# A transformer block on one core: attention outputs turned in 32x32 squares on VectorE instead of on TensorE, and the cross output projection moved into the next period

## What is computed

```python
def _attn(x, ctx, wq, wk, wv, wo, bo, heads):
    q = (x @ wq).reshape(b, n, heads, dh).transpose(0, 2, 1, 3)
    k = (ctx @ wk)...; v = (ctx @ wv)...
    a = jax.nn.softmax(jnp.einsum('bhid,bhjd->bhij', q, k) * scale, axis=-1)
    out = jnp.einsum('bhij,bhjd->bhid', a, v).transpose(0, 2, 1, 3).reshape(b, n, heads * dh)
    return out @ wo + bo
h1 = _ln(x, n1_g, n1_b); x = _attn(h1, h1, q1, k1, v1, o1_w, o1_b, heads) + x
h2 = _ln(x, n2_g, n2_b); x = _attn(h2, context, q2, k2, v2, o2_w, o2_b, heads) + x
h3 = _ln(x, n3_g, n3_b); a, g = split(h3 @ ff_w1 + ff_b1, 2)
return a * gelu(g) @ ff_w2 + ff_b2 + x
```

## Time and profile before

| what | value |
|---|---|
| median of three runs | 1340.88 us |
| the profiled execution: its span | 1337.6 us |
| TensorE busy / weight loads | 1292.3 us (97%) / 1203.1 us (90%) |
| VectorE busy | 814.5 us (61%) |
| ScalarE busy | 673.2 us (50%) |
| GpSimd busy | 612.5 us (46%) |
| a period of the attention part | 24.89 us, 29 of them |

### The profile page before, as it was taken

The page is one execution under the profiler, slowest core; times in us unless marked ns, Lnnn a source line. Parts: engine busy times, 40 slices in busy tenths (PEclk is TensorE's granted clock), DMA queues, the critical chain, the costliest instruction groups (busy, mean ns, idle before and its releaser), DMA issues. The chain is left out here.

```text
span 1337.6 us, 35594 instructions
## 1 busy us (share of the span) xinstructions
PE 1292.3 (97%) x13364; PEld 1203.1 (90%) x13364; DVE 814.5 (61%) x1729; ACT 673.2 (50%) x1558; POOL 612.5 (46%) x723
## 2 busy tenths in 40 slices
PE   5999789999999999999999999999889999999999
PEld 3999769999999999999999999998689999999999
DVE  5645367777777777777777777776665334242421
ACT  4665236566566566566566565565553232313131
POOL 5521324564564564654654654644356242333331
PEclk8999889999999999999999999999899999999999
DMA  4676644345345455455444354352111101010000
GB/s 125 223 253 215 206 130 145 116 147 153 120 142 155 141 158 162 142 162 166 134 148 149 121 162 132 122 157 95 42 56 48 45 1 50 0 49 0 25 1 25
DMA packets 118995, 154.59 MB, mean 116 GB/s; under 512 B 22336, under 2 KB 112696, under 8 KB 118840
## 3 DMA queue, kind: packets, MB, share of 16 engines
q1 hardware_dynamic: 118840, 152.49, 36.9%
HBM read 62.98 MB, written 28.93 MB: 69 GB/s over the span
## 5 line engine op out<-in xcount | busy, mean ns | idle before, releaser
L1398 ACT ACTIVATE probs<-expin 120x400 f32<-120x400 f32 (+2 forms) x635 | 297.8, 505 | 119.1 <-PE expin L753 106.4
L1075 DVE TENSOR_REDUCE neg_max<-score 100x2 f32<-100x722 f32 x320 | 289.6, 905 | 61.6 <-PE score L727 59.7
L1584 POOL MEMSET qs<- 1x2400 f32 (+1 forms) x116 | 224.2, 1933 | 17.2 <-PE attn L776 9.4
L753 PE MATMUL expin<-qs,ks 128*120 128x200 f32 (+2 forms) x1270 | 216.0, 276 | 2.6 <-ACT probs L1398 1.7
L753 PEld LDWEIGHTS expin<-qs,ks 128*120 128x120 f32 (+2 forms) x1270 | 178.0, 180 | 14.2 <-issue 4.4
L727 PE MATMUL score<-ks,qs 128*100 128x362 f32 x640 | 167.5, 343 | 6.0 <-DVE neg_max L1075 4.7
L1612 POOL TENSOR_TENSOR ctx_hi<-ctx_raw,one 128x480 fp32r<-128x480 f32 (+1 forms) x62 | 49.0, 790 | 260.2 <-PE work L693 239.8
L2594 DVE SCALAR_TENSOR_TENSOR hidden<-ps_a,b_cols,gelu 128x320 f32<-128x320 f32 x100 | 55.1, 551 | 163.5 <-PE ps_a L2518 159.1
L2756 POOL TENSOR_TENSOR hid_lo<-hidden,hid_hi 128x320 fp32r<-128x320 f32 x100 | 89.1, 892 | 120.6 <-ACT hid_hi L2664 120.4
L2676 ACT ACTIVATE gelu<-ps_g,b_cols 128x320 f32<-128x320 f32 x100 | 52.7, 527 | 134.3 <-PE ps_g L2518 134.3
L727 PEld LDWEIGHTS score<-ks,qs 128*100 128x100 f32 x640 | 84.8, 166 | 23.3 <-issue 8.7
(11 more groups left out here) (220 smaller groups left out, 2965.3 us busy)
## 6 DMA issues: line engine op xcount, KB each, us to landing
ks<-kc_parts SPq DMA_DIRECT2D x192, 181.0 KB, 2.8
qk_dram<-qk_parts SPq DMA_DIRECT2D x32, 500.0 KB, 5.3
qs<-q_parts SPq DMA_DIRECT2D x192, 75.0 KB
ks<-qk_dram SPq DMA_DIRECT2D x96, 125.0 KB
ctx_raw<-in_ctxT SPq DMA_DIRECT2D x64, 180.5 KB
ks<-kc_parts SPq DMA_DIRECT2D x96, 90.5 KB, 2.3
qs<-qk_dram SPq DMA_DIRECT2D x64, 125.0 KB
v_dram<-v_rows SPq DMA_DIRECT2D x32, 132.8 KB
```

What stands on the lines that cost most here:

```text
L753: mm = pe.matmul(dst, ks[a][u][:, c, j0:j0 + n], qs[a][u][:, :, q_slot(c) if a == 2 else c, :], start=True, stop=True)
L1075: ins = nc.vector.tensor_reduce(dst, src, AX_X, ALU.max, negate=True)
L1398: nc.scalar.activation(probs[e % NPT][0:n, :], expin[e % 2][0:n, 0:HG * N], ACT.Exp, scale=SCALE)\
L1584: link(nc.gpsimd.memset(row, 0.0))
```

## The change

The two turns on TensorE are gone. `copy_heads` on ScalarE copies `attn` in two instructions (400 and twice 100 columns) into a tile of 128 x 640, so that the columns fall into squares of 32. VectorE turns each 32x32 square of it (`turn_heads`, 640 columns) and takes 20 reciprocals; GpSimd multiplies (`scale_products`, 320 columns); VectorE turns the squares back (`turn_back`, 320 columns). The result has features in partitions, with the heads in another order, and ScalarE and GpSimd split it into high and low parts (`heads_high` from SBUF, `heads_low`). One set of these tiles serves both attentions in turn. The rows of the output weights are loaded in the new order of heads (`head_rows`, 24 DMAs of each of two matrices instead of 3), and the first stage turns the first item's heads the same way.

The cross output projection of x moves from the end of its period to the front of the next (`y = x - 1`), ahead of the second own score; `result` and `store_x2` move with it. The own output projection and keys part 1 change places, and so do the matching steps on VectorE. GpSimd clears a whole stack with one instruction instead of two rows with two, and SP's loads into the stack wait for that. In the drain the split of the feed-forward's weights stands behind the heads of the last items.

```diff
+def copy_heads(nc, pv, attn):
+    src = attn[:, 0:4 * N].rearrange("p (k s n) -> p k s n", k=2, s=2)
+    dst = pv[:, :, 0:4 * N - N].rearrange("p s (k n) -> p k s n", n=N)[:, 0:3:2]
+    nc.scalar.copy(dst, src)
+    last = attn[:, 4 * N:5 * N].unsqueeze(1).broadcast_to([P, 2, N])
+    return nc.scalar.copy(pv[:, :, N:2 * N], last)
+def scale_heads(engine, scaled, turned, rden):
+    src = turned[:].rearrange("p (s b r) -> p b s r", s=2, r=BLK)[:, :, :, 0:DH]
+    factor = rden[:].rearrange("p (s b) -> p b s", s=2).unsqueeze(3).broadcast_to([P, NB_HW, 2, DH])
+    return engine.tensor_tensor(scaled[:].rearrange("p (b s d) -> p b s d", s=2, d=DH), src, factor, ALU.mult)
...
 # TensorE, period
+                y = x - 1 if x else None
                 self_scores(f, 0)
...
                 scores_for_exp(1, c, 3, 0)
+                project_out(2, y)
                 self_scores(f, 1)
...
                 scores_for_exp(2, x, 0, 1)
-                turn_outputs(1, c, 0)
                 turn_max(1, f)
                 scores_for_exp(2, x, 0, 2)
-                turn_outputs(1, c, 1)
                 scores_for_exp(2, x, 1, 0)
...
                 times_v(2, x, 0)
-                turn_heads(1, c)
                 scores_for_exp(2, x, 1, 2)
                 scores_for_exp(2, x, 2, 0)
                 cross_scores(s, 2)
-                project_out(1, c)
+                project_kc(c, 1)
                 scores_for_exp(2, x, 2, 1)
                 scores_for_exp(2, x, 2, 2)
                 cross_scores(s, 3)
-                project_kc(c, 1)
+                project_out(1, c)
                 scores_for_exp(2, x, 3, 0)
                 scores_for_exp(2, x, 3, 1)
                 project_kc(c, 2)
                 cross_scores(s, 4)
...
                 project_q2(c)
-                turn_outputs(2, x, 0)
                 cross_scores(s, 7)
                 project_vc(c, 1)
-                turn_outputs(2, x, 1)
                 turn_q2(c)
                 cross_scores(s, 8)
-                turn_heads(2, x)
                 project_vc(c, 2)
                 cross_scores(s, 9)
-                project_out(2, x)
                 turn_max(2, s)
 # VectorE
-            def divide(a, b, i):
...
+            def turn_heads(a, b):
...
+                dve.wait_ge(pv_copied, n + 2)
+                dve.wait_ge(heads_lo_made, n + 1)
+                m = link(nc.vector.transpose(turned[:], pv[:].rearrange("p s c -> p (s c)")))
+                dve.wait_ge(dve_step, m)
+                invert_sums(nc, rden, turned).then_inc(heads_turned, 1)
+            def turn_back(a, b):
...
+                dve.wait_ge(heads_scaled, n + 1)
+                nc.vector.transpose(dense[:], scaled[:]).then_inc(heads_dense, 1)
 # VectorE, period
                 kc_low(c, 0)
+                result(y)
                 maximum(2, s, 0)
-                divide(1, c, 0)
-                divide(1, c, 1)
+                turn_heads(1, c)
                 maximum(2, s, 1)
                 max_low(1, f)
-                features_low("OT1", c)
+                turn_back(1, c)
                 maximum(2, s, 2)
+                kc_low(c, 1)
                 second_input(c)
                 maximum(2, s, 3)
                 normalise(c)
                 maximum(2, s, 4)
-                kc_low(c, 1)
                 maximum(2, s, 5)
...
                 maximum(2, s, 6)
-                divide(2, x, 0)
+                turn_heads(2, x)
                 maximum(2, s, 7)
-                divide(2, x, 1)
                 maximum(2, s, 8)
                 q2_low(c)
-                features_low("OT2", x)
+                turn_back(2, x)
                 maximum(2, s, 9)
                 max_low(2, s)
-                result(x)
 # ScalarE
             def heads_high(a, b):
...
+                act.wait_ge(heads_dense, n + 2)
+                before = OUT_BEFORE.get(n - 1, (1, 0))
+                act.wait_ge(*filled((f"O{before[0]}", before[1], 0)))
+                nc.scalar.copy(t_hi["OT"][:], thirds_of_heads(dense)).then_inc(heads_hi_made, 1)
 # GpSimd, run_out
+                scale_products(2, 31)
+                heads_low(2, 31)
                 for i in range(EARLY):
                     split_piece(i)
 # GpSimd, period
+                scale_products(1, c)
+                heads_low(1, c)
                 clear_own(p + 4 if p + 4 < B else None)
                 inverse_deviation(c)
-                split_context(f)
-                clear_cross(c)
                 second_residual(c)
                 first_residual(f)
+                clear_cross(c)
+                scale_products(2, x)
+                split_first(f)
+                heads_low(2, x)
+                split_last(f)
 # SP, first stage
+            def head_rows(dst, w, done):
+                for p0, k, src in rows_of_heads(w):
+                    sp.dma_start(dst[p0:p0 + DH, k, :], src).then_inc(done, 16)
```

More of the change, by code:

```diff
@@ L105 @@
 OWN_STEPS = [("scores", 0), ("scores", 1), ("max", 0)] + [("exponents", g) for g in range(G)]
-OWN_STEPS += [("values", g) for g in range(G)] + [("outputs", 0), ("outputs", 1), ("heads", 0)]
+OWN_STEPS += [("values", g) for g in range(G)]
 OWN_FULL = {step: n + 1 for n, step in enumerate(OWN_STEPS)}
 PROBS_AT, INPUT_AT = 27552, 43904
+LEAD_ROOM = 128
 @dataclass
@@ L209, with rows_of_heads @@
 PV_AT = {job: i for i, job in enumerate(PV)}
+CLEARED = [job for p in PERIODS for job in ((1, p + 4), (2, p + 2)) if job[1] < B] + [(2, B - 1)]
+CLEARED_AT = {job: i + 1 for i, job in enumerate(CLEARED)}
+HEADS_AT = {(a, b): i // G for (a, b, g), i in PV_AT.items() if g == 0}
+OUT_BEFORE = {n: (a, b) for (a, b), n in HEADS_AT.items()}
 def thirds_of(w):
     return [w[0:P], w[P:C].unsqueeze(0).broadcast_to([2, 64, w.shape[1]])] + ([w[C:D]] if w.shape[0] == D else [])
+def rows_of_heads(w):
+    pieces = []
+    for k, f0, step in ((0, 0, 4 * DH), (2, P, 4 * DH), (1, 2 * P, 0)):
+        for i in range(HG):
+            for half in range(2):
+                f = f0 + half * step + DH * i
+                pieces.append((BLK * i + DH * half, k, w[f:f + DH]))
+    return pieces
 def rows3(w):
@@ L652, in project_q2 @@
                     return
-                project(("Q2", b, 0), "T2", ("T2", b, 0), (hi_made["T2"], b + 1), [w_q2[:, i, :] for i in range(6)])
+                project(("Q2", b, 0), "T2", (hi_made["T2"], b + 1), emptied(("T2", b, 0)), [w_q2[:, i, :] for i in range(6)])
             def turn_q2(b):
@@ L1403, in copy_product @@
                     return
+                n = HEADS_AT[a, b]
                 act.wait_ge(pv_made, PV_AT[a, b, G - 1] + 1)
-                if b > (a == 1):
-                    act.wait_ge(*filled((f"OX{a}", b - 1, 1)))
-                nc.scalar.copy(pv[a][:], attn[:, 0:G * N]).then_inc(pv_copied, 1)
+                if n:
+                    act.wait_ge(heads_turned, n)
+                else:
+                    act.wait_ge(keys_set, 32)
+                copy_heads(nc, pv, attn).then_inc(pv_copied, 1)
             def heads_high(a, b):
@@ L1579, in inverse_deviation, with clear_stack @@
                 nc.gpsimd.tensor_tensor(rstd[:], var_eps[:], neg_half[0:N, :], ALU.pow).then_inc(rstd_made, 1)
-            def clear_rows(stack, landed):
-                for r in (0, 64):
-                    row = stack[r:r + 1].rearrange("p a c n -> p (a c n)").bitcast(F32)
-                    link(nc.gpsimd.memset(row, 0.0))
+            def clear_stack(stack, landed):
+                link(nc.gpsimd.memset(stack.rearrange("p a c n -> p (a c n)").bitcast(F32), 0.0))
+                pool.sem_inc(max_cleared, 1)
                 pool.sem_inc(landed, 16)
@@ L1929, in own_values @@
                 mm.then_inc(own_full, 1)
-            def turn_outputs(i):
-                pe.wait_ge(pv_copied, 1)
-                c0, c1 = XB[i]
-                for c in range(c0, c1):
-                    mm = pe.transpose(turn[i][0:N, (c - c0) * P:(c - c0 + 1) * P], ahead.pv[:, c * N:(c + 1) * N], identf[:])
-                mm.then_inc(own_full, 1)
-            def turn_heads():
-                pe.wait_ge(heads_made, 2)
-                pe.wait_ge(qk_lo_made, LAST + 1)
-                for k in range(3):
-                    mm = pe.transpose(qk_ps[2][:, k * N:(k + 1) * N], ahead.oh[:, k * P:(k + 1) * P], identf[0:N, 0:N])
-                mm.then_inc(own_full, 1)
             def turn_max():
@@ L1986, in _ @@
             values(NK - 1, 0)
-            for i in range(2):
-                turn_outputs(i)
-            values(NK - 1, 1)
-            values(NK - 1, 2)
-            turn_heads()
-            values(NK - 1, 3)
+            for i in range(1, NB):
+                values(NK - 1, i)
         @block.vector
@@ L2152, in _ @@
                 if k == NK - 1:
-                    for i in range(2):
-                        divide(i)
+                    normalise_heads()
                     heads_low()
@@ L2351, in _ @@
             pool.wait_ge(lo_made, B)
```

(1 more changed line is left out.)

259 lines of the change are left out of this document (133 added, 126 removed), and 8 rows, old and new, of tables (DRAIN_WORK, FILL_WORK).

## The result

The changed kernel took 1478.21 us in the median of four runs (1477.44 to 1483.67), the kernel before 1338.45 in the same series. The ratio is 1.107, with a 95% interval of 1.103 to 1.110. The profiled execution has a span of 1475.5 us against 1337.6, so 137.9 us more. They lie here, by the starts of the turn of the cross maxima that ends each period: 4.6 us more until the first of them (192.11 against 187.50), 114.1 more in the 29 periods (840.8 against 726.7), 17.8 more from there to the feed-forward (81.9 against 64.1), and 1.4 in the feed-forward.

A forecast was written before the change was run, and what follows sets the result against it. TensorE's list was taken to bound the 29 periods. Terms sum to +2.79 us a period, +81, plus 10.5 in the drain and 2 in the first stage: +94, giving 1434 us; range 1378 to 1485.

The forecast's parts named there:

- turns removed from TensorE: TensorE's list in each period: two turns to items by rows and one to features, per attention, go; -1.66 us.
- end of the period: Product 6 to next own scores: product and maximum rounds lack cover, 6.54 us against 4.95 of work; +1.76 us (1.59 to 2.1).
- maximum 3 behind the second input: Middle of the period: TensorE waits ahead of product 4, as VectorE's second input waits for the own output projection; +1.09 us.
- ScalarE's front: Front half of the period: split copy and wait at the heads' high parts make exponentials late; +0.9 us (0 to 1.4).
- normalisation beside GpSimd: VectorE's normalisation overlaps GpSimd's moved second residual sum, so maximum 4 is late; +0.30 us (0 to 0.47) a period.
- context's last piece: GpSimd's last context split stands behind the heads' low parts, so the keys part needing it waits; +0.40 us (0 to 1).
- the clock falls: Rival: new waits bring the 1.2 GHz level in half the periods, 3.25 us each, +47, 1481 us; chance 0.09.
- The drain: After the periods: GpSimd's feed-forward weight split stands behind the last heads and delays the next stage; +10.5 us (0 to 14).
- The lead-in: First stage: TensorE loses some 0.8 us and SP issues 48 pieces of weights instead of 6; +2 us (-1 to 8).
- Floors only: Rival: turns hide, ScalarE's, GpSimd's and normalisation's terms are nothing; +1.02 us a period, about 1382 us; chance 0.12.
- Slow turns: Rival: a VectorE 32x32 turn takes twice the assumed 0.80 and 0.40 us; +58, 1492 us; chance 0.09.
- Faster: Rival: TensorE stays full, deciding at 1.05 us a product and maximum round; -48 in the periods, 1305 us; chance 0.05.

The follow-up runs named there:

- own products early: Against the changed kernel with all new orders together: next item's own exponent products 0 to 3 and own values 0 and 1 moved into the period's end; 1383.99 us.
- the front's two more orders: Against the kernel with own products early: keys part 0 behind the second own score, second cross exponent product ahead of product 0; 1391.29 us.

## Why the prediction was right, and where it was short

The direction, the mechanism and the range held; the time was 44 us above the forecast of 1434. By the profiles these are 25.6 us of slow clock, 12.5 in the periods' terms (29 times the 0.43 between 3.22 and 2.79), 7.3 in the drain, 2.6 in the lead-in and 1.4 in the feed-forward, less 4.9 since the periods before were longer than 24.89 in sum. By the prediction's own steps, for an undisturbed period:

| step | predicted us | measured us | from |
|---|---|---|---|
| turns removed from TensorE | -1.66 | -1.66 | taken from the earlier trace rows |
| end of the period | +1.76 | +1.89 | 336.58 - 329.74 = 6.84 for 4.95 of work |
| maximum 3 behind the second input | +1.09 | +1.05 | wait at 324.69 |
| ScalarE's front | +0.9 | +1.05 | 320.76 - 315.22 = 5.54 for 4.49 of work |
| normalisation beside GpSimd | +0.30 | +0.29 | products 4 to 6: 5.05 against 4.76 |
| context's last piece | +0.40 | +0.57 | own scores to keys: 1.87 against 1.30 |
| sum | +2.79 | +3.19 | 28.11 - 24.89 = 3.22 |

The own scores that end the period began at 336.58. The 4.49 us of work are the 5.72 between the same products before, less two turns and a third (0.84) and the output projection (1.22) and with keys part 1 (0.83).

- **The removed turns** did come out of TensorE's list, and the 1.66 us were more than lost again, because the list had to wait elsewhere. The floor of 1.59 at the period's end was the right reading of the earlier trace rows: rounds of 1.58 us in a single score bank; the stretch lost 1.89.
- **The turns' durations** came out near the row chosen: 0.83 and 0.50 us against 0.80 and 0.40. The Trainium skill, VectorE: DVE Perf Modes, section The three transpose paths, gives 311 ns for 128 columns; taken in proportion this gave 1.56 and 0.78, which the trace refutes. From 0.83 and 0.50 one works out 1.03 ns a column and 0.17 us that don't grow with them; by these 128 columns of float32 would take some 0.30 us, an estimate near the page's figure, which is for bf16; so it was the proportion that was wrong.
- **A turn made longer by GpSimd's work**, for which the prediction named up to +3.7 us a period, did not occur: all 63 turns of 640 columns in the attention part took 823 to 845 ns and all 63 of 320 columns 499 to 516. The normalisation became longer, 0.94 us instead of 0.48; before it did so in two places, not one (178.81 and 926.72), each beside the residual sum.
- **The step that was short** is the rival "the clock falls". It was priced at 3.25 us in half the periods and given a chance of 9 in 100, because the lead-in had had more waits just before. It happened, in 15 of 29 periods. Its cost, 840.8 - 29 x 28.11 = 25.6 us, and the 93.4 us of 29 x 3.22 are the two parts of the periods, less the 4.9 us by which the periods before were above 24.89 themselves. The case that came true was this rival together with the main sum, 1481 by the prediction, and that 1478 lies so near to it is luck: the slow clock cost 25.6 us and not 47, and the other terms made up for it. The lead-in's row should have weighed more: it showed the very sequence, a wait of 1.10 us at the same turn of the maxima, then half the clock, and the changed kernel repeats this wait in each period. Why the clock fell in 15 of them and not in the other 14, which have the same waits, no run shows.
- **The drain** was priced at 10.5 us and took 17.8. The splits' part was right (8.4 us more of idle time; moving them gave 7.8). The other 9.4 lie in the stretch ahead, where the granted clock is 0.90 until 1082 and 0.74 from there to 1104.2 (before: 1.00 until 954.1, then 0.86 to the feed-forward) and TensorE waits for maxima and heads; which part each has was not separated.
- **The lead-in** cost 4.6 us against 2: the first output projection starts 3.3 us later (150.29 against 146.99), and SP's last store of the values ends 3.3 us later too (149.71 against 146.42), its list being longer by the pieces of the weights. This was read from the two timelines, not tried by a run.
- "Floors only" put ScalarE's, GpSimd's and the normalisation's terms at nothing; they came to 1.91 us a period.
- "Slow turns" would have cost 2 us a period by the prediction; the run with each turn done twice cost 2.86.
- "Faster" failed on its deciding point: a round took 1.55 to 1.9 us in the rows above, never near 1.05 (products 6 to 9 and the turn of the maxima).

## What to carry to other kernels

Work on the engine that sets the pace can be worth less than its duration: what it hides is part of its value, and before removing or moving it one asks which chain (here product, maximum, product in one bank) has to fit into what is left. A rival that one row has shown, here a wait and then half the clock, is added to the sum when the change repeats that row's sequence in every period. And in lists worked in order, the instruction behind a late one is late too: each wait went to the place that the lists named, and a swap that freed one maximum only bound the next.

## What was not expected of the hardware

Products that nobody reads made the kernel 29 us faster, by holding TensorE's clock at 2.4 GHz through a wait that stayed as long. GpSimd cleared 128 rows of 2400 columns in 2.10 us, while before two single rows of the same length took 4.25 together: clearing a whole stack cost no more than clearing one row of it. Before, then after:

```profile
540.15 4.25 POOL L1584 MEMSET qs<- 1x2400 f32 x2
327.41 2.10 POOL L1603 MEMSET qs<- 128x2400 f32 x1 [0.98 <-PE expin L811]
```

The same clear, started 0.15 us ahead of a normalisation on VectorE, made that take 2.15 us instead of 0.48; where it started 0.2 us or more behind, the normalisation kept its 0.48 (runs with own products early and with the front's two more orders).
